# GCN passes of a graph network: from pairs to quads of node tiles, with neighbour sums formed feature-major

## What is computed

```python
h = relu(((1 + eps) * x + segment_sum(relu(x[src] + edge_attr @ W_edge + b_edge), dst)) @ W1 + b1) @ W2 + b2
x = layernorm(x + relu(batchnorm(h)))
def layer(h, W, b):                      # norm = dinv[src] * dinv[dst], with self loops
    h = h @ W.T
    agg = segment_sum(h[src] * norm[:, None], dst, num_segments=n)
    return relu(agg + b)
x = layernorm(x + layer(layer(layer(x, W1, b1), W2, b2), W3, b3))
```

## Time and profile before

| | us |
|---|---|
| median of 3 runs | 4458.0 (4437.5 to 5123.0) |
| profiled execution, own time | 4450.0 |
| its span | 4448.3 |
| PE busy | 3981.7 (90%) |
| DVE busy | 3717.4 (84%) |
| ACT busy | 2647.1 (60%) |
| POOL busy | 2234.4 (50%) |
| mean DMA rate | 205 GB/s |

### The profile page before, as it was taken

The page is one execution under the profiler, slowest core; times in us unless marked ns, Lnnn a source line. Parts: engine busy times, 40 slices in busy tenths (PEclk is TensorE's granted clock), DMA queues, the critical chain, the costliest instruction groups (busy, mean ns, idle before and its releaser), DMA issues. The chain is left out here.

```text
span 4448.3 us, 107968 instructions
## 1 busy us (share of the span) xinstructions
PE 3981.7 (90%) x27934; PEld 3560.4 (80%) x27934; DVE 3717.4 (84%) x10652; ACT 2647.1 (60%) x6276; POOL 2234.4 (50%) x1972
## 2 busy tenths in 40 slices
PE   6559999999999997999978889887898887999999
PEld 1149999999999986888868888886888887888887
DVE  8737777777777768999968888886888886999999
ACT  0015555555555556888857877775787776344444
POOL 0044444444444410000057777767777775777776
PEclk9869999999999998999989999998999999999999
DMA  0154444444444428999966767665677766999998
GB/s 23 2 108 136 137 137 135 135 136 135 137 135 136 136 75 294 375 374 375 375 193 210 217 206 213 207 192 176 213 217 210 213 211 186 294 311 310 311 310 285
DMA packets 871189, 909.87 MB, mean 205 GB/s; under 512 B 154170, under 2 KB 770580, under 8 KB 871060
## 3 DMA queue, kind: packets, MB, share of 16 engines
q1 hardware_dynamic: 744400, 702.74, 48.3%
...
## 5 line engine op out<-in xcount | busy, mean ns | idle before, releaser
L460 POOL DMA_INDIRECT rows<-ga_scratch,node_i x980 | 1092.1, 1114 | 1005.8 <-POOLq L596 707.6
L460 POOL DMA_INDIRECT rows<-x_in,node_i x490 | 567.4, 1158 | 812.4 <-DVE raw L913 617.7
L460 POOL DMA_INDIRECT rows<-gb_scratch,node_i x490 | 571.6, 1167 | 181.5 <-issue 169.4
L488 PE MATMUL gcn_agg_ps<-gcn_rows_hi,gcn_select 128*128 128x256 f32 x2156 | 580.0, 304 | 33.6 <-DVE gcn_rows_lo L1258 33.6
L488 PE MATMUL gcn_agg_ps<-gcn_rows_lo,gcn_select 128*128 128x256 f32 x2156 | 546.9, 288 | 0.0
L860 ACT ACTIVATE h1t_hi<-h1t_ps,b_sb 128x256 fp32r<-128x256 f32 x392 | 164.3, 470 | 628.9 <-issue 493.6
L1378 PE MATMUL fin_agg_ps<-rows,fin_select 128*128 128x256 f32 x2156 | 530.9, 380 | 0.0
L1277 ACT CAST gcn_rows_hi<-rows 128x768 fp32r<-128x768 f32 (+1 forms) x392 | 286.3, 731 | 332.3 <-DMA rows<-gb_scratch,node_i 161.9
L1378 PEld LDWEIGHTS fin_agg_ps<-rows,fin_select 128*128 128x128 f32 x2156 | 411.0, 191 | 56.3
L488 PEld LDWEIGHTS gcn_agg_ps<-gcn_rows_hi,gcn_select 128*128 128x128 f32 x2156 | 421.9, 196 | 34.6 <-DVE gcn_rows_lo L1258 34.6
L515 PE MATMUL gcn_g_ps<-g_hi,gcn_ht_hi 128*128 128x256 f32 x1568 | 444.0, 283 | 0.7 <-ACT gcn_g L1296 0.7
...
## 6 DMA issues: line engine op xcount, KB each, us to landing
own<-x_in SPq DMA_DIRECT2D x196, 256.0 KB, 2.6
h_scratch<-h2t SPq DMA_DIRECT2D x196, 256.0 KB, 2.0
h2t_in<-h_scratch SPq DMA_DIRECT2D x196, 256.0 KB, 3.8
x_sb<-x_in SPq DMA_DIRECT2D x196, 256.0 KB, 4.8
x_scratch<-x SPq DMA_DIRECT2D x196, 256.0 KB, 4.9
ga_scratch<-g_out SPq DMA_DIRECT2D x196, 256.0 KB, 5.0
gcn_own<-ga_scratch SPq DMA_DIRECT2D x196, 256.0 KB
gb_scratch<-gcn_g SPq DMA_DIRECT2D x196, 256.0 KB, 3.4
```

The source lines that it names most:

```text
L460: pool.indirect_dma_start(out=c["rows"][:, slot, b], out_offset=None, in_=source[:, :], in_offset=bass.IndirectOffsetOnAxis(ap=c["node"][: ...
L488: last = nc.tensor.matmul(out[:, j], select[:, b, j * P:(j + 1) * P], rows[:, pair.odd + b], start=n == 0, stop=n == len(terms) - 1)
```

## The change

Both GCN passes work on quads. The bias no longer comes in after the scaling: with r = root of the degree, relu(dinv * s + b) * dinv = relu(s + b * r) * dinv * dinv, so DVE forms `own_b` = bias * r + own row (four instructions per quad), PE transposes `own_b` into the accumulator, and the sums follow into the same accumulator, feature by node: now the rows are the loaded operand and `select` streams, 128 to 384 columns at a time (`SPAN`). ACT's relu reads the accumulator and writes `ht_hi` at once, DVE's one instruction forms `ht_lo` from the accumulator and `ht_hi`. `total`, `scaled`, `ht` and `ht_ps` are gone, and the last scaling uses `dinv2`, one over the degree. `rows_hi` and `rows_lo` are formed by one instruction of 1280 elements each, the second by a scalar-tensor-tensor operation. `root` and `dinv2` are kept from the degree stage, at the cost of one more reciprocal. The store lags the load by 6 quads.

```diff
@@ degrees
-                nc.vector.tensor_scalar(root2[:], root2[:], 0.5, None, ALU.mult).then_inc(chain, 1)
+                nc.vector.tensor_scalar(c["root"][:], root2[:], 0.5, None, ALU.mult).then_inc(chain, 1)
+                nc.vector.reciprocal(c["dinv2"][:], deg1[:])
@@ new helpers
+SPAN = [(0, 2), (0, 3), (1, 4), (2, 4), (3, 4)]
+def select_columns(nc, c, quad, select):
+    for b, (first, end) in enumerate(SPAN):
+        last = nc.vector.tensor_scalar(select[:, b, 0:(end - first) * P], c["iota32"][:, first * P:end * P],
+                                       c["place"][:, bass.ds(quad.q, 1), b], None, ALU.is_equal)
+    return last
@@ gather_quads
-            pool.wait_ge(rows_free, 2 * (quad - QUAD_RING) + 2)
+            pool.wait_ge(rows_free, (quad - QUAD_RING + 1) * per)
@@ gcn_pass, sync
-                    if pair := at(11):
+                    if quad := at(0):
+                        load_quad(sp, fast, own[:, quad.slot], source, dram["base"], quad, loaded[quad.slot], own_ready)
+                    if quad := at(6):
+                        sp.wait_ge(g_ready, quad.done())
+                        sp.dma_start(quad_rows(target, quad.q), g[:, quad.slot]).then_inc(stored[quad.slot], 16)
@@ gcn_pass, tensor
-                    if pair := at(6):
-                        transpose_rows(nc, c, ht_ps[:, b], scaled[:, b]).then_inc(h_turned, 1)
-                    if pair := at(3):
-                        sum_into_nodes(nc, pair, agg_ps[:, b], select[:, b], [rows_hi[:, half], rows_lo[:, half]])\
...
-                    if pair := at(9):
+                    if quad := at(4):
+                        b = quad.b
+                        pe.wait_ge(h_split, quad.done())
+                        if quad.has(2):
+                            pe.wait_ge(g_ready, quad.before(2))
+                        terms = [(h, a, w) for h in range(2) for a, w in products([ht_hi[:, b], ht_lo[:, b]], weight)]
+                        for j in range(4):
+                            for n, (h, a, w) in enumerate(terms):
+                                last = nc.tensor.matmul(g_ps[:, b, j], a[:, h, j * P:(j + 1) * P], w[:, h],
+                                                        start=n == 0, stop=n == len(terms) - 1)
+                        last.then_inc(dense_done, 1)
+                    if quad := at(2):
+                        b = quad.b
+                        pe.wait_ge(own_ready, quad.done())
+                        if quad.has(2):
+                            pe.wait_ge(h_split, quad.before(2))
+                        for h in range(2):
+                            for j in range(4):
+                                nc.tensor.matmul(agg_ps[:, b, h, j * P:(j + 1) * P],
+                                                 own_b[:, b, j, h * P:(h + 1) * P], c["ident"][:], start=j == 0,
+                                                 stop=False, is_transpose=True, skip_group_check=True)
+                        pe.wait_ge(rows_split, quad.done())
+                        pe.wait_ge(select_done, quad.done())
+                        for k, (first, end) in enumerate(SPAN):
+                            for h in range(2):
+                                for rows in (rows_hi, rows_lo):
+                                    last = nc.tensor.matmul(agg_ps[:, b, h, first * P:end * P],
+                                                            rows[:, b, k, h * P:(h + 1) * P],
+                                                            select[:, b, k, 0:(end - first) * P], start=False,
+                                                            stop=k == BLOCKS - 1 and rows is rows_lo,
+                                                            skip_group_check=True)
+                        last.then_inc(agg_done, 1)
@@ gcn_pass, vector
-                        nc.vector.tensor_tensor(total[:, b], agg_ps[:, b], own[:, s], ALU.add).then_inc(total_done, 1)
-                        nc.vector.tensor_copy(ht_hi[:, b], ht[:, b]).then_inc(h_split, 1)
-                        nc.vector.tensor_tensor(rows_lo[:, half, blocks], c["rows"][:, pair.quad_slot, blocks],
-                                                rows_hi[:, half, blocks].bitcast(F32), ALU.subtract)\
-                        nc.vector.tensor_tensor(ht_lo[:, b], ht[:, b], ht_hi[:, b].bitcast(F32), ALU.subtract)\
...
+                    if quad := at(3):
+                        b = quad.b
+                        dve.wait_ge(h_rounded, quad.done())
+                        nc.vector.scalar_tensor_tensor(out=ht_lo[:, b], in0=agg_ps[:, b], scalar=0.0,
+                                                       in1=ht_hi[:, b].bitcast(F32), op0=ALU.max,
+                                                       op1=ALU.subtract).then_inc(h_split, 1)
+                    if quad := at(1):
+                        b, s = quad.b, quad.slot
+                        if quad.has(2):
+                            dve.wait_ge(agg_done, quad.before(2))
+                        dve.wait_ge(loaded[s], quad.landed(1))
+                        for j in range(4):
+                            last = nc.vector.scalar_tensor_tensor(out=own_b[:, b, j], in0=bias[:],
+                                                                  scalar=c["root"][:, quad.tile(j)], in1=own[:, s, j],
+                                                                  op0=ALU.mult, op1=ALU.add)
+                        last.then_inc(own_ready, 1)
+                        select_columns(nc, c, quad, select[:, b]).then_inc(select_done, 1)
+                        dve.wait_ge(rows_rounded, quad.done())
+                        nc.vector.scalar_tensor_tensor(out=rows_lo[:, b], in0=c["rows"][:, s], scalar=1.0,
+                                                       in1=rows_hi[:, b].bitcast(F32), op0=ALU.mult,
+                                                       op1=ALU.subtract).then_inc(rows_split, 1)
@@ gcn_pass, scalar
-                            last = nc.scalar.activation(ht[:, b, h], ht_ps[:, b, h], ACT.Relu, bias=bias[:, h:h + 1])
-                            last = nc.scalar.activation(scaled[:, b, j], total[:, b, j], ACT.Identity,
...
+                    if quad := at(3):
+                        b = quad.b
+                        act.wait_ge(agg_done, quad.done())
+                        if quad.has(2):
+                            act.wait_ge(dense_done, quad.before(2))
+                        nc.scalar.activation(ht_hi[:, b], agg_ps[:, b], ACT.Relu).then_inc(h_rounded, 1)
+                    if quad := at(1):
+                        b, s = quad.b, quad.slot
+                        act.wait_ge(gathered[s], quad.landed(BLOCKS))
+                        if quad.has(2):
+                            act.wait_ge(agg_done, quad.before(2))
+                        nc.scalar.copy(rows_hi[:, b], c["rows"][:, s]).then_inc(rows_rounded, 1)
+                    if quad := at(5):
+                        s = quad.slot
+                        act.wait_ge(dense_done, quad.done())
+                        if quad.has(QUAD_RING):
+                            act.wait_ge(stored[s], quad.turn * 16)
+                        for j in range(4):
+                            last = nc.scalar.activation(g[:, s, j], g_ps[:, quad.b, j], ACT.Identity,
+                                                        scale=c["dinv2"][:, quad.tile(j)])
                         last.then_inc(g_ready, 1)
```

191 lines of the change are left out of this document (74 added, 117 removed).

## The result

The changed kernel takes 4472.8 us (median of 9 runs), the kernel before 4449.3 in the same comparison: ratio **1.0057**, interval 1.0042 to 1.0071. I had forecast 4420 and a gain of 33 us on the profiled execution; it lost 26 us, from 4450.0 to 4476.0. The time is inside the range and inside "within 2%", but the sign is wrong. Of the nine runs of each kernel one lay far above the others (8941.9 and 5123.0 us), and the ratio leaves it out.

The account below looks back on a forecast made before the run. POOL's gather issue was taken to bound the GCN passes, 7.40 us per quad falling to 7.30; -19 for gathers, -17 for pass ends, +3 for the reciprocal gave -33 us on 4450, i.e. 4417, put at 4420; range 4325 to 4540.

Parts of the forecast that it names:

- The bound: GCN passes: POOL's issuing of gathers sets the pace, 7.40 us per quad; shorter ACT and PE chains worth 0.
- The rule of the hold: A gather starting under a DVE instruction with two SBUF inputs ends 0.87 us after it; `ht_lo`, reading PSUM, holds none.
- One in every quad: GCN passes: `rows_lo`, longer than the 1.30 us between gather starts, catches one gather in every quad, costing 0.0 to 1.32 us.
- `rows_lo` at 1.48 us, `own_b` and `select` at 0.15 us together: DVE in GCN passes: `rows_lo` takes 1.48 us; gathers under `own_b` and `select` lose 0.15 us per quad together.
- Where the one caught gather stands: Walk of one GCN quad: `rows_lo` holds the fourth gather for 0.65 us, the fifth is free; 7.3 us per quad.
- the landing: Time from a quad's last gather's end to ACT's copy of its rows, taken as 2.32 us, the old kernel's median.
- the forecast's own cases: GCN passes: landings of 1.97 to 2.78 us give 6.95 to 7.75 us per quad, 4350 to 4508 us.
- the fourth gather caught early: Rival, GCN passes: 512 KB transfers delay landing to 2.95 us, fourth gather loses 1.3; 7.96 per quad, 4549 us; chance 0.15.
- The bytes per quad are the same: Argument against the rival in which longer landing catches the fourth gather early: the change moves as many bytes per quad.
- Ends: Ends of both GCN passes: shorter drains gain 8.5 us per pass, 17 in all; the second reciprocal costs 2.6 us.
- The drain of 19 us: GCN pass end: from last gather to last stores issued, 19 us instead of 28.0.
- The reciprocal: Degree stage: one more reciprocal costs 2.6 us with nothing beside it, entered as +3 in the sum.

Follow-up runs that it names:

- small loads: Changed kernel, own-row load cut to one tile of four in first GCN pass (store likewise in second), output wrong; 4741.3 us, ratio 0.9766 to kernel before.
- the halves: Changed kernel with own rows loaded and results stored as two 256 KB transfers instead of one of 512 KB; 4459.2 us, ratio 1.0025 to kernel before.

## Why the prediction was wrong

By its own steps:

- *The bound.* Right: the passes ran at the rate of the gathers, ACT's and PE's shorter lists were worth 0, and ACT's freed time became waiting.
- *The rule of the hold.* Right: 0.87 us behind the end, for `rows_lo` in either form, none for `ht_lo` with its PSUM input. "One in every quad" is right as well (195 gathers under 196 `rows_lo`).
- *`rows_lo` at 1.48 us, `own_b` and `select` at 0.15 us together.* Measured 1.49, and 0.15, though an `own_b` took 0.48 us and not 0.41.
- **Where the one caught gather stands. This step failed.** It took the landing, 2.32 us, from the kernel before and left it there. In the changed kernel it is 3.14, and in two heaps, near 2.6 and near 3.9 us, instead of one. An early landing (median 2.55 us of 76 quads) puts `rows_lo` just ahead of the fourth gather, which loses 1.15 us on average, a late one (3.75, 107 quads) ahead of the fifth, which loses 0.74; the two held gathers of the timeline are one of each. The heaps go with the hold itself: where the last gather of a quad had been held, its landing was early (median 2.71 us, 105 quads), where it had not, late (3.79, 89 quads). The term is 0.89 instead of 0.65 us, and 6.51 + 0.15 + 0.89 = 7.55, where 7.56 was measured. Over 196 quads that is +31 us in place of -19, 50 of the 59 us by which the forecast missed. 7.56 lies inside the forecast's own cases, 6.95 to 7.75, because they let the landing vary; the value in the middle, and with it the sign, did not hold.
- *Its rival, the fourth gather caught early.* The mechanism I named is at least part of what happened: the 512 KB transfers lengthen the landing. The small loads (1.47 us against 3.13, few quads, on a pausing chip) and the halves (3.14 to 2.76, -14 us) bear it out; the halves leave 0.44 us of the lengthening unexplained. Its price of 1.3 in every quad was too high, since a landing of 3.9 us, beyond the 3.64 I had as the longest, lets the fourth gather by and meets the fifth. "The bytes per quad are the same", my argument against it, did not hold: with the same bytes per quad in transfers of half the size the landing was shorter.
- *Ends.* The drain of 19 us and the -17 us are right to a microsecond. The reciprocal, put at 3 us, was 1.6.
- *Left out.* The GIN and norm passes took 9.4 us more. They are unchanged code; the part of it that is the change's, by the place of the tiles, is between 0 and 7 us, and the runs leave it open.

The Trainium skill (page "SBUF — State Buffer", section "Who interferes with whom") infers that `tensor_tensor` takes only the read side of the shared port pair and so leaves descriptor generation alone, beside a statement that with both inputs in SBUF it contends with GpSimd's reads. Taken as in my prediction, that a gather would not be held, the inference is refuted here: 194 of 196 gathers under the `tensor_tensor` form of `rows_lo` ended 0.87 us behind it, as did 194 of 195 under the scalar-tensor-tensor form, and the times are the same, ratio 1.0060 for 1.0057. Which side of the pair the gather waits for, no run here shows.
